# A chunked linear recurrence on one core: input stored by position in the chunk, and the output's two products split around the scan

## What is computed

```python
h = _rmsnorm(x, norm_w)
u = h @ Win + b_in
u = causal_conv4(u, conv_w) + conv_b        # per channel, 4 taps
def step(hc, u_t):
    hc = jnp.einsum('bdr,drs->bds', hc, A) + u_t[:, :, None] * Bv[None]
    y = jnp.einsum('bds,ds->bd', hc, Cv)
    return (hc, y)
_, ys = jax.lax.scan(step, h0, u.transpose(1, 0, 2))
return y @ Wout + b_out + res
```

## Time and profile before

| | us |
|---|---|
| median of 3 executions | 2330.77 |
| lowest, highest | 2330.49, 2334.44 |
| the profiled execution, its own time | 2336.39 |
| its span | 2334.7 |
| recurrence (stages 1 to 8), to about | 346 |
| projection, about | 346 to 440 |

### The profile page before, as it was taken

One profiled execution on the slowest core, in us unless ns is written; L12 is line 12 of the kernel. 1 busy time (PEld: TensorE's weight loads), 2 busy tenths in 40 slices (PEclk: granted clock), 3 DMA queues, 4 the chain that ended last, 5 costly groups with the idle time before them and its releaser, 6 DMA issues. The chain is left out here.

```text
span 2334.7 us, 28969 instructions
## 1 busy us (share of the span) xinstructions
PE 1848.8 (79%) x8208; PEld 1433.9 (61%) x8208; DVE 1405.6 (60%) x3320; ACT 998.7 (43%) x1840; POOL 891.1 (38%) x795
## 2 busy tenths in 40 slices
PE   8999996479999999997577657767689984443699
PEld 7999993257777777775455435545466652222487
DVE  6412224467666666665457657757665558997566
ACT  5302012145445554543455435524377762222454
POOL 5601101035555555554000035510068873221265
PEclk9899587689999999998567678879889996665799
DMA  2001000176545555543000045410011101000455
GB/s 61 2 1 20 1 1 7 25 161 146 115 108 108 116 106 120 108 108 68 19 1 1 2 91 108 90 36 1 1 46 38 43 18 27 1 1 1 82 120 123
DMA packets 114094, 129.92 MB, mean 56 GB/s; under 512 B 40262, under 2 KB 58826, under 8 KB 114026
## 3 DMA queue, kind: packets, MB, share of 16 engines
q1 hardware_dynamic: 112216, 128.65, 25.9%
q10 hardware_dynamic: 1810, 0.42, 0.1%
HBM read 125.51 MB, written 3.54 MB: 55 GB/s over the span
## 5 line engine op out<-in xcount | busy, mean ns | idle before, releaser
L800 POOL TENSOR_TENSOR ffn_alo<-ffn_a,ffn_ahi 128x512 fp32r<-128x512 f32 x520 | 670.5, 1292 | 507.8 <-ACT ffn_ahi L761 504.1
L827 DVE TENSOR_TENSOR ffn_a<-ffn_G,ffn_mask 128x512 f32<-128x512 f32 x384 | 264.7, 689 | 238.1 <-ACT ffn_G L769 216.7
L769 ACT ACTIVATE ffn_G<-ffn_G 128x512 f32<-128x512 f32 x384 | 223.5, 582 | 355.6 <-PE ffn_G L116 353.3
L761 ACT ACTIVATE ffn_ahi<-ffn_a 128x512 fp32r<-128x512 f32 x520 | 324.6, 624 | 32.4 <-DVE ffn_a L831 29.0
L114 PE MATMUL ypsum<-ffn_ahi,ffn_hi 128*128 128x512 f32 x520 | 227.7, 438 | 51.3 <-POOL ffn_alo L800 37.0
L114 PE MATMUL ffn_G<-xn_hi,ffn_hi 128*128 (+1 forms) x520 | 220.3, 424 | 29.9 <-DVE ffn_lo L807 27.1
L831 DVE TENSOR_TENSOR ffn_a<-ffn_U,ffn_a 128x512 f32<-128x512 f32 x320 | 221.4, 692 | 30.1 <-DVE ffn_a L827 1.0
L115 PE MATMUL ffn_G<-xn_lo,ffn_hi 128*128 (+1 forms) x520 | 214.6, 413 | 0.0
L116 PE MATMUL ffn_G<-xn_hi,ffn_lo 128*128 (+1 forms) x520 | 214.3, 412 | 0.0
L115 PE MATMUL ypsum<-ffn_alo,ffn_hi 128*128 128x512 f32 x520 | 209.8, 404 | 0.0
L116 PE MATMUL ypsum<-ffn_ahi,ffn_lo 128*128 128x512 f32 x520 | 208.9, 402 | 0.0
(11 more groups left out here) (551 smaller groups left out, 3709.9 us busy)
## 6 DMA issues: line engine op xcount, KB each, us to landing
ffn_mask<-mask_rows_top SPq DMA_DIRECT2D x128, 512.0 KB, 6.9
ffn_mask<-mask_rows_top SPq DMA_DIRECT2D x16, 1024.0 KB, 8.3
ffn_mask<-mask_rows_zone SPq DMA_DIRECT2D x16, 1024.0 KB, 8.3
ffn_mask<-mask_rows_steps SPq DMA_DIRECT2D x16, 512.0 KB, 4.9
x<-in_L_attn_x SPq DMA_DIRECT2D x8, 256.0 KB, 4.8
ffn_raw<-in_L_ffn_expert_gate_k SPq DMA_DIRECT2D x16, 128.0 KB, 4.0
ffn_raw<-in_L_ffn_expert_up_k SPq DMA_DIRECT2D x16, 128.0 KB, 4.1
ffn_raw<-in_L_ffn_expert_down_k SPq DMA_DIRECT2D x16, 128.0 KB, 4.4
```

The lines of the kernel that those rows point to most:

```text
L761: act.activation(ahi[i][:, :], a[i][:, :], ACT.Copy).then_inc(k.ahi_done, 1)
L769: act.activation(gate if masked(c) else a[c % RING_A][:, :], gate, how, **kw).then_inc(k.r_done, 1)
L800: eng.tensor_tensor(alo[i][:, :], a[i][:, :], ahi[i][:, :].bitcast(F32), ALU.subtract).then_inc(k.alo_done, 1)
L827: dve.tensor_tensor(out, gate[:, :], mask(c), ALU.mult).then_inc(k.t_done, 1)
```

## The change

- `A` is loaded block by block from DRAM into zeroed memory, by 8 DMAs on SP, which wait until DVE and POOL have zeroed it. The multiplications by a mask go. ACT's queue loads `compact` and, by 8 more DMAs, repeated rows of C; DVE forms the vector A C from them, from which C's powers now start.
- With that, stage 3's extra power goes. DVE multiplies A^k B by C (`lc`, 128x1024), and two products with an 8-column mask, 512 columns wide, give the impulse responses.
- `xn_hi` and `xn_lo` are stored by position: all 128 chunks' tokens of one position lie side by side. `hi` and `rest` read PSUM with a step for it; the stationary operand of stage 4 is contiguous.
- The products inside the chunk (`near`) are issued between the scan's groups, into banks of their own; ACT copies them to `Y`. The carried state's products (`far`) follow the scan, 256 columns wide, and DVE adds each bank to `Y`.
- In the projection DVE's order becomes: addition, statistics and their aggregate of group g; choice of experts of g-1; `xn_tokens` and `xn_lo` of g.

```diff
+def by_place(t, g):
+
+    each = GROUP // CHUNK
+    return t[:, 0:TOKENS].rearrange("p (j q) -> p j q", q=P)[:, :, g * each:(g + 1) * each]
+
+
+def from_tokens(bank):
+    return bank[:, :].rearrange("p (q j) -> p j q", j=CHUNK)
+
+
+def chunk_ends(t, d):
+    return t[:, (CHUNK - d) * P:(CHUNK - d + 1) * P].rearrange("p (b n) -> p b n", n=CHUNKS)[:, :, 0:CHUNKS - 1]
...
-        sp.dma_start(s.compact, io["L0_attn_A"].rearrange("(g c) r s -> (c r) g s", c=PACK)).then_inc(ev["a_in"], 16)
+        sp.wait_ge(ev["a_zero"], 2)
+        blocks = io["L0_attn_A"].rearrange("(g c) r s -> c r g s", c=PACK)
+        for c in range(PACK):
+            at = slice(ST * c, ST * (c + 1))
+            sp.dma_start(s.A[at, :, at], blocks[c]).then_inc(ev["a_in"], 16)
...
-            pe.wait_ge(ev["bd_d" if q < 4 else "bd_p"], q % 4 + 1)
+            if q == 0:
+                pe.wait_ge(ev["a_in"], 16 * PACK)
...
+        pe.wait_ge(ev["ac_done"], 1)
...
-        for p in range(PACKS):
-            last = pe.matmul(k.turn[:, p:p + 1], A[:, p, 0:P], AT[:, p, P:P + 1], start=True, stop=True)
-        last.then_inc(ev["l32_psum"], 1)
-        pe.wait_ge(ev["cbd"], 1)
-        for p in range(PACKS):
-            out = (k.ypsum, bank[4])[p // 16]
-            last = pe.matmul(out[0:PACK, p % 16 * CHUNK:(p % 16 + 1) * CHUNK], s.cbd[:, p, :], AT[:, p, P:P + CHUNK],
-                             start=True, stop=True)
-            if p % 16 == 15:
-                last.then_inc(ev["k_psum"], 1)
+        pe.wait_ge(ev["lc_done"], 1)
+        for i, out in enumerate((k.ypsum, bank[4])):
+            pe.matmul(out[0:PACK, :], s.mask8[:, :], s.lc[:, 16 * i:16 * i + 16, :].rearrange("p g n -> p (g n)"),
+                      start=True, stop=True).then_inc(ev["k_psum"], 1)
...
-                        x = [t[:, j - m:TOKENS:CHUNK] for t in (k.xh, k.xl)]
+                        x = [t[:, (j - m) * P:(j - m + 1) * P] for t in (k.xh, k.xl)]
...
+        ybank = (bank[0], bank[1], bank[2], k.ypsum)
+
+        def near(r):
+            pe.wait_ge(ev["t0_done"], r + 1)
+            if r >= 4:
+                pe.wait_ge(ev["y_near"], r - 3)
+            for u in range(4):
+                last = pe.matmul(ybank[r % 4][:, u * P:(u + 1) * P], s.U2[:, 4 * r + u, :],
+                                 s.T0[:, 4 * r + u, :, :].rearrange("p c j -> p (c j)"), start=True, stop=True)
+            last.then_inc(ev["near_psum"], 1)
+
+        def far(r):
+            if r == 0:
+                pe.wait_ge(ev["h_zero"], 1)
+                pe.wait_ge(ev["sc_done"], SUBS * (CHUNKS - 2))
+                pe.wait_ge(ev["y_near"], 16)
+            pe.wait_ge(ev["f_done"], r + 1)
+            if r >= 4:
+                pe.wait_ge(ev["y_done"], r - 3)
+            for i in range(2):
+                p = 2 * r + i
+                last = pe.matmul(ybank[r % 4][:, i * 2 * P:(i + 1) * 2 * P], s.H[:, p, :],
+                                 s.F[:, p, :, :].rearrange("p c j -> p (c j)"), start=True, stop=True)
+            last.then_inc(ev["y_psum"], 1)
+
+        done = 0
         for n in range(1, CHUNKS - 1):
             for sub in range(SUBS):
                 if n > 1:
@@ -2230,31 +2263,16 @@
                     last = pe.matmul(out[:, i * BATCH:(i + 1) * BATCH], A[:, p, 0:P], s.H[:, p, n:P:CHUNKS],
                                      start=True, stop=True)
                 last.then_inc(ev["sc_psum"], 1)
-
+                if (SUBS * (n - 1) + sub) * 16 // 24 >= done:
+                    near(done)
+                    done += 1
+        assert done == 16
         for r in range(16):
-            if r == 0:
-                pe.wait_ge(ev["h_zero"], 1)
-                pe.wait_ge(ev["sc_done"], SUBS * (CHUNKS - 2))
-            pe.wait_ge(ev["t0_done"], r + 1)
-            pe.wait_ge(ev["f_done"], r + 1)
-            if r >= 4:
-                pe.wait_ge(ev["y_dve" if r % 2 else "y_act"], (r - 4) // 2 + 1)
-            out = (bank[0], bank[1], bank[2], k.ypsum)[r % 4]
-            for i in range(2):
-                p = 2 * r + i
-                for half in range(2):
-                    at = i * 2 * P + half * P
-                    pe.matmul(out[:, at:at + P], s.U2[:, 2 * p + half, :],
-                              s.T0[:, 2 * p + half, :, :].rearrange("p c j -> p (c j)"), start=True, stop=False)
-                    last = pe.matmul(out[:, at:at + P], s.H[:, p, :],
-                                     s.F[:, p, QUAD * half:QUAD * (half + 1), :].rearrange("p c j -> p (c j)"),
-                                     start=False, stop=True)
-            last.then_inc(ev["y_psum"], 1)
+            far(r)
...
-            pe.wait_ge(ev["y_act"], 4 * t + 4)
-            pe.wait_ge(ev["y_dve"], 4 * t + 4)
+            pe.wait_ge(ev["y_done"], 8 * t + 8)
...
+        act.dma_start(s.compact, k.io["L0_attn_A"].rearrange("(g c) r s -> (c r) g s", c=PACK)).then_inc(ev["ac_in"], 16)
+        for c in range(PACK):
+            src = bass.AP(k.io["L0_attn_Cm"].tensor, ST * c, [[0, ST], [ST * PACK, PACKS], [1, ST]])
+            act.dma_start(s.crep[ST * c:ST * (c + 1), :, :], src).then_inc(ev["ac_in"], 16)
...
-            copy(tokens(k.xh, g), (k.turn, k.ypsum)[g % 2][:, :]).then_inc(ev["hi"], 1)
+            copy(by_place(k.xh, g), from_tokens((k.turn, k.ypsum)[g % 2])).then_inc(ev["hi"], 1)
...
+        for r in range(16):
+            act.wait_ge(ev["near_psum"], r + 1)
+            if r == 8:
+                act.wait_ge(ev["t0_done"], 16)
+            copy(s.Y[r // 8][:, r % 8 * 16:r % 8 * 16 + 16, :].rearrange("p c j -> p (c j)"),
+                 (bank[0], bank[1], bank[2], k.ypsum)[r % 4][:, :]).then_inc(ev["y_near"], 1)
+        finish_y(s, act, copy, "yc_act", 0)
...
+        dve.memset(A[:, 0:16, 0:P], 0.0).then_inc(ev["a_zero"], 1)
...
+        dve.wait_ge(ev["ac_in"], 16 * (PACK + 1))
+        dve.tensor_tensor(s.crep, s.crep, s.compact, ALU.mult).then_inc(ev["ac_mul"], 1)
+        dve.wait_ge(ev["ac_mul"], 1)
+        dve.tensor_reduce(A[:, :, P], s.crep, AX_X, ALU.add).then_inc(ev["ac_done"], 1)
...
-            dve.tensor_tensor(tokens(k.xl, g), turn[g % 2][:, :], tokens(k.xh, g).bitcast(F32), ALU.subtract)\
+            dve.tensor_tensor(by_place(k.xl, g), from_tokens(turn[g % 2]), by_place(k.xh, g).bitcast(F32), ALU.subtract)\
...
+        dve.tensor_tensor(s.lc, AT[:, :, P:P + CHUNK], s.ccol.unsqueeze(2).to_broadcast([P, PACKS, CHUNK]), ALU.mult)\
+           .then_inc(ev["lc_done"], 1)
...
-        finish_y(k, s, dve, dve.tensor_copy, 1)
+        for r in range(16):
+            dve.wait_ge(ev["y_psum"], r + 1)
+            y = s.Y[r // 8][:, r % 8 * 16:r % 8 * 16 + 16, :].rearrange("p c j -> p (c j)")
+            dve.tensor_tensor(y, y, (bank[0], bank[1], bank[2], k.ypsum)[r % 4][:, :], ALU.add).then_inc(ev["y_done"], 1)
+        finish_y(s, dve, dve.tensor_copy, "yc_dve", 1)
...
-        for q in range(4, 8):
-            pool.tensor_tensor(A[:, 4 * q:4 * q + 4, 0:P].rearrange("p g (c s) -> p g c s", c=PACK),
-                               s.compact[:, 4 * q:4 * q + 4, :].unsqueeze(2).to_broadcast([P, 4, PACK, ST]),
-                               s.mask[:, :, :].unsqueeze(1).to_broadcast([P, 4, PACK, ST]), ALU.mult)\
-                .then_inc(ev["bd_p"], 1)
...
-                    p.part(0, post, 2)
+                    p.part(0, post, 20, 21, 22, 23)
                     p.part(1, post, 13)
-                    p.part(0, post, 6)
+                    p.part(0, post, 24, 25, 6)
```

More of the change, by code:

```diff
@@ L76, in share @@
     k.tick2 = k.sb("tick_gpsimd", [P, 1])
+    k.tick_norm = k.sb("tick_norm", [P, 1])
     k.yT = k.sb("y_features", [P, GROUP])
@@ L2015, in carve @@
         self.bc = take(2, P)
-        self.cbd = take(PACKS, PACK)
+        self.crep, self.ccol = take(PACKS, ST), take(PACKS)
+        self.lc = self.mix[:, 0:PACKS * CHUNK].rearrange("p (g n) -> p g n", n=CHUNK)
         self.h = [take(GT, D) for _ in range(2)]
@@ L2263, in _, with finish_y @@
             last.then_inc(ev["yt_turned"], 1)
-def finish_y(k, s, eng, copy, parity):
-    ev = s.ev
-    names = ("y_act", "yc_act") if parity == 0 else ("y_dve", "yc_dve")
-    for r in range(parity, 16, 2):
-        eng.wait_ge(ev["y_psum"], r + 1)
-        if r >= 8:
-            eng.wait_ge(ev["t0_done"], 16)
-        out = (s.bank[0], s.bank[1], s.bank[2], k.ypsum)[r % 4]
-        copy(s.Y[r // 8][:, r % 8 * 16:r % 8 * 16 + 16, :].rearrange("p c j -> p (c j)"), out[:, :]).then_inc(ev[names[0]], 1)
+def finish_y(s, eng, copy, name, parity):
     for r in range(parity, 16, 2):
         t, first = r // 8, r % 8 * 4
-        eng.wait_ge(ev["yt_turned"], r + 1)
-        out = (s.bank[3], s.bank[4], s.bank[5], k.turn)[r % 4]
+        eng.wait_ge(s.ev["yt_turned"], r + 1)
+        out = (s.bank[3], s.bank[4], s.bank[5], s.turn)[r % 4]
         to = s.yc[:, t, :].rearrange("p (q j) -> p q j", j=CHUNK)[:, :, first:first + 4]
-        copy(to, out[:, :].rearrange("p (i q) -> p q i", i=4)).then_inc(ev[names[1]], 1)
```

(26 more changed lines are left out.)

43 lines of the change are left out of this document (14 added, 29 removed).

## The result

The changed kernel takes 2319.28 us, the median of 6 runs (2317.88 to 2322.86); the kernel before, run beside it, 2335.64 (6 runs, 2330.49 to 2343.88). The ratio is 0.9924, 95% interval 0.9902 to 0.9947: some 16 us shorter. The profiled execution took 2322.86 us, with a span of 2321.1; PE was busy 1810.7 us in 8020 instructions.

What follows compares the result with a forecast made beforehand. PE's time per instruction was taken as the bound up to the projection, a chain through DVE there. Five terms (+4, -10.5, -40.3, +14, +12) sum to -20.8: 2315.6 from the profiled execution, forecast as 2310, range 2252 to 2324 us.

Steps and rivals of the forecast that it cites:

- the sum: Whole program: five terms, 4 - 10.5 - 40.3 + 14 + 12 = -20.8 us, from the profiled 2336.39 to 2315.6.
- likeliest case: Whole program: the prediction's own case of all five terms, chance 0.70, spanning 2298 to 2324 us.
- Start, +4: Before the rounds: zeroing and A's eight DMAs delay the rounds from 15.4 to 19.3 us; bounds 0 and +8.
- Rounds, nothing: Rounds: PSUM reads stepping 32 elements in the hi and rest copies costed at nothing, at most +2.4 us.
- Between rounds and stage 4, -10.5: Between rounds and stage 4: lc and four wide instructions replace 64 one-column instructions, saving 10.5 us, bounds 9 and 13.
- Stage 4, -40.3: Stage 4: contiguous xn_hi columns cut 366 products from 0.223 to 0.113 us each, saving 40.3 us, bounds 36 and 42.
- The rival: Stage 4: the 0.22 us spacing is not the stride's, so 40.3 us are not saved; sum 2350, chance 0.04.
- Scan and output, +14: Scan and output: near adds 27.3 us at the lower clock, far adds 16.3, the 29.4 us output stage goes.
- the rival with the upper clock: Scan: it keeps the upper clock, giving -38.4 us instead of +14; sum 2258, chance 0.19.
- Projection, +12: Projection: choice still waits for the sigmoid, xn comes behind; +1.9 us in seven turns, taken as 12, bounds 0 and 15.
- The rival's rule on the clock: Scan: the skill's rule that keeping TensorE continuously busy holds the full clock, cited for the upper-clock rival, chance 0.19.

Runs made afterwards that it cites:

- old turn: Changed kernel with the old order of DVE's steps in the projection's turn restored, nothing else: 2308.7 us.
- 64 columns: Changed kernel with the scan's narrow products streaming 64 columns instead of 16, 48 of the results unused: 2274.0 us.
- token storage: Changed kernel with xn_hi and xn_lo stored by token again, stationary operand's columns 32 elements apart: 2357.1 us.
- near behind: Changed kernel with the 64 near products moved out of the scan, as one block between scan and far products: 2309.0 us.
- POOL behind `lc`: Changed kernel with POOL's expansions made to wait for DVE's lc, nothing else changed: 2319.4 us.
- masked start: Changed kernel with A again loaded as one compact DMA and multiplied by the mask, without zeroing and eight block DMAs: 2312.7 us.
- first combination: Changed kernel, with projection's old DVE order, 64-column scan, compact masked A, expansions behind lc, casts in round 39, kernels' product after stage 4's first group: 2269.0 us.
- second combination: The first combination with DVE's extra work in the rounds cut up: aggregation in four parts, weights in eight, casts singly in rounds 48 to 53: 2252.1 us.

## Why the prediction was right, and where it was off

The direction, the stages and their mechanisms were right: 2310 was forecast and 2319.3 measured, inside the range. Against the profiled execution the sum was 2315.6, measured 2322.9. Of the 9.3 us between the medians, 4.9 are the starting point: the forecast counts from 2330.77, the median of three executions, and six give 2335.64. The other 4.4 are the sum's own, -20.8 against -16.4 up to the eighth addition, and that it is so little is in part luck: terms that came out 8.6 us too long (start, rounds, the stretch to stage 4, stage 4) stand against 4.2 too short (scan, projection, and the 0.5 us ahead of its first addition).

The upper end of the range, 2324, lies higher than the prediction's own working puts it. Half of each bound that the prediction names, added, is 10 us down and 8 up, so 2300 to 2318 for the likeliest case and not 2298 to 2324; the scan's term has no bound at all. 2319.3 lies just outside that. By its terms:

- **Start, +4:** measured +4.95. Right in kind, near by luck. I had the eight issues' end at 7.7 (9.08) and overlooked that PE's first instruction needs `Bm` and `Cm`, issued behind them: 3.1 us too early. But the 32 transpositions took 4.9 us, not 7.2. I had read 0.28 us each from four in 1.12, where the end of the last is counted in: both kernels start them 0.21 us apart at first and 0.11 later on (and my own figures, 12 at 0.28 and 20 at 0.17, give 6.8). With the masked load the whole term is gone.
- **Rounds, nothing:** measured +1.65. My bound of +2.4 was for slower copies out of PSUM; that was the wrong cause, they take what they took. It is a short fall of the clock, to the lower level for 3.4 us from 42.2, after DVE's weights hold PE up for 2.55 us. It comes and goes: PE stands the same 2.55 us in the kernel before, where the clock stayed up. Of the experiments with the same rounds, they took 80.1 us at 1.00 in two (old turn, 64 columns), and 81.7 to 81.8 with the dip in four (token storage, near behind, POOL behind `lc`, masked start). So it is no cost of the change; why the clock falls in some executions is open.
- **Between rounds and stage 4, -10.5:** measured -6.4, the one term outside its bounds (9 to 13 saved). The step that failed is "DVE's last copies for `before`, done at 96.57": I took the 0.62 us for three from the trace of before and did not ask what sheltered them. I had written that DVE and POOL no longer wait for L2150; that very release let POOL's expansions in beside the casts, which then took 5.9 us instead of 1.1. `lc` went the other way: 1.21 us, not the 2.2 that I took from an expansion made beside POOL, since POOL had just finished.
- **Stage 4, -40.3:** measured -38.4; the first 1.1 us at the lower clock, and a spacing of 0.118, not 0.113. The mechanism is shown by undoing it alone (+38). The rival is out.
- **Scan and output, +14:** measured +12.9. 512 instructions at the lower clock took what they should, and the rival with the upper clock did not come. That it was the clock and not the products is shown twice: outside the scan they cost 17 us instead of 29, and with more columns the scan takes 58.
- **Projection, +12:** measured +9.35, by the mechanism described: the choice waited for the sigmoid (2.67 us), `xn` and its tail came behind. The term is too large because only six of the seven turns that it counts grew. The first of the turns between the eight additions holds no choice of experts and stayed at 9.4 us, and behind the eighth addition the router product came no later than before (8.70 us after it, 9.35 before). The six grew by 0.6 to 3.2 us, 1.6 on average, not by 1.9; the turn shown grew by 2.05. The old order alone gives it back.
- **The rival's rule on the clock.** In the scan of the changed kernel PE is 99% busy for 107 us at 0.52. The Trainium skill (TensorE: Matmul & The Clock Gate, "Why this matters for your kernels") would have the clock up there; as worded it does not hold for narrow products, in this kernel as in the one before.

## What to carry to other kernels

PE being 99% busy says nothing about its clock: read PEclk for each stage, and where products are so narrow that the weight load sets their time, stream more columns of what lies there anyway; in these two kernels it cost nothing and gained 39 and 45 us. Before costing work that moves into a slow stage, ask at which clock it will run there, and before taking a wait away, which other engine was standing still behind it. A gap on PE can cost twice, once for itself and once for the clock behind it (2.55 us and then 1.65 in the rounds of the changed kernel), so work on another engine in a tight loop is better cut into pieces of the idle time that each round has.

## What the runs showed that was not expected

**The margin of 64 columns.** In the scan with 64 columns the clock stayed at 1.00 in three kernels, but fell near its start in two, the first and the second combination. Windows of the scan's first 24 us in the second:

```profile
178.00:186.00 8.00, 7.93 (x46) 7.93 (x47) 2.12 (x5) 0.60 (x1) 8.00 (x8) 0.63 0.00 0
186.00:194.00 8.00, 8.00 (x55) 8.00 (x54) 3.50 (x5) 1.20 (x2) 5.50 (x7) 0.73 0.01 2
194.00:202.00 8.00, 8.00 (x74) 8.00 (x73) 2.99 (x7) 1.20 (x2) 0.00 (x0) 1.00 0.00 0
```

It came back by itself while the scan ran, which it never did with 16 columns (107 us at 0.52). It cost 4.9 us there (63.2 us for the scan instead of 58.3) and 1.7 in the first combination. Before the scan PE stands 0.9 us for DVE in all of them; why it fell in two of the five was not tried.

**The unchanged rest.** From the projection's first product to the end, the profiled executions with the new turn took 1989 to 2006 us (six kernels, mean 1995), those with the old turn 1976 to 1994 (six, mean 1986). The difference of the means agrees with the turn's 9 us; the spread of 17 and 18 us is in code that is the same in all of them, with the same instruction count, and goes with the granted clock (a mean of 0.834 in the longest, 0.845 in the shortest). So a local gain of 5 us, as that of POOL's wait, can be proved in its stretch and still be invisible in the total.

**The company of POOL.** A cast of 112 columns on DVE took 0.16 us alone, 1.0 beside POOL's expansions (1.0 us each) and 2.3 when it met one of its multiplications for the bias (2.2 to 2.4 us each), though the two engines share no data. It takes the length of the POOL instruction that it meets, whatever its own.
